# Last stage of a two-layer decoder: linears and quantised tiles batch by batch within a pair, the next pair's context part between them, bias rows added to residuals ahead of time

## What is computed

```
x = LN(x)                                              # norm 3 of the stage
x = LN1(x + Wo (Wv x + bv) + bo)                       # self-attention, whose mask leaves the diagonal; norm 4
x = LN2(x + Wm softmax(q k^T / sqrt(32)) v + bm)       # 8 heads over the context, k and v from ctx; norm 5
x3 = LN3(x + W2 relu(W1 x + b1) + b2)                  # 1024 hidden units, norm 6
x = LN(residual + x3)                                  # norm 7
gate, up = bitlinear(x, w_gate), bitlinear(x, w_up)    # 8-bit activations, ternary weights
x = LN(x + bitlinear(silu(gate) * up, w_down))         # norm 8, stored
```

## Time and profile before

| | us |
|---|---|
| median of 3 runs | 4651.4 (4647.05 to 4660.06) |
| the profiled execution | 4649.78 |
| its span | 4648.1 |
| what lies around the span | 1.7 |
| mean granted clock of PE, share of full | 0.946 |
| last stage, from the end of the state-space part (3946.5) to the end of the span | 701.6 |
| busy over the span: PE, DVE, ACT, POOL | 85%, 67%, 50%, 49% |

### The profile page before, as it was taken

The page is one execution under the profiler, slowest core; times in us unless marked ns, Lnnn a source line. Parts: engine busy times, 40 slices in busy tenths (PEclk is TensorE's granted clock), DMA queues, the critical chain, the costliest instruction groups (busy, mean ns, idle before and its releaser), DMA issues. The chain is left out here.

```text
span 4648.1 us, 46710 instructions
## 1 busy us (share of the span) xinstructions
PE 3953.6 (85%) x14986; PEld 2031.9 (44%) x14992; DVE 3108.6 (67%) x4273; ACT 2307.0 (50%) x4217; POOL 2283.4 (49%) x1206
## 2 busy tenths in 40 slices
PE   7888888888868997589999999999999987785785
PEld 3434434433438997233333333333333333434433
DVE  3464565455462111299999999999999998546546
ACT  3454444444442222476666666666666663432432
POOL 2353343344340001477877787878887785220220
PEclk9999999999989999799999999999999998898998
DMA  6000000000017886111111111111111120000000
GB/s 217 19 1 15 19 5 10 19 5 10 10 54 306 312 313 250 49 32 37 47 35 39 35 40 44 35 39 34 47 35 39 35 91 31 1 1 19 9 1 9
DMA packets 102377, 272.86 MB, mean 59 GB/s; under 512 B 9777, under 2 KB 55729, under 8 KB 96401
## 3 DMA queue, kind: packets, MB, share of 16 engines
q1 hardware_dynamic: 97216, 256.75, 16.1%
q0 software_dynamic: 4944, 13.51, 0.8%
HBM read 237.32 MB, written 32.90 MB: 58 GB/s over the span
## 5 line engine op out<-in xcount | busy, mean ns | idle before, releaser
L742 POOL TENSOR_TENSOR AR<-AR 128x1024 f32<-128x1024 f32 x512 | 1216.5, 2382 | 415.6 <-DVE AR L1852 339.1
L1852 DVE TENSOR_TENSOR_SCAN AR<-AR,PS 128x1024 f32<-128x1024 f32 x512 | 1170.6, 2286 | 17.6
L641 POOL TENSOR_TENSOR AR<-AR,rden 128x1024 f32<-128x1024 f32 x320 | 605.7, 1893 | 1121.7 <-DVE rden L1615 1055.5
L1385 PE MATMUL PS<-AR,ident 128*128 128x512 f32 x2048 | 1023.4, 627 | 32.2 <-POOL AR L742 31.7
L1005 ACT ACTIVATE AR<-AR,mcol 128x511 f32<-128x511 f32 x1024 | 668.0, 712 | 140.5 <-DVE AR L1852 138.1
L1846 DVE TENSOR_TENSOR PS<-AR,PS 128x1024 f32<-128x1024 f32 x512 | 628.1, 1227 | 78.6 <-PE PS L1370 59.6
L1385 PEld LDWEIGHTS PS<-AR,ident 128*128 128x128 f32 x2048 | 371.3, 194 | 479.2 <-issue 412.3
L1159 PE MATMUL PS<-ident,AR 128*128 128x128 f32 x2560 | 344.9, 278 | 122.1 <-issue 66.9
L1159 PEld LDWEIGHTS PS<-ident,AR 128*128 128x128 f32 x2560 | 276.5, 142 | 381.2 <-issue 360.5
L1147 PE MATMUL PS<-AR 64*128 64x512 f32 x1280 | 364.5, 650 | 50.9 <-ACT AR L806 24.0
L806 ACT ACTIVATE AR<-PS,nm 128x512 f32<-128x512 f32 x384 | 260.1, 683 | 295.4 <-DVE nm L1595 219.2
(11 more groups left out here) (266 smaller groups left out, 4726.2 us busy)
## 6 DMA issues: line engine op xcount, KB each, us to landing
AR<-in_xw SPq DMA_DIRECT2D x39, 3072.0 KB, 10.5
AR<-mid_cs SPq DMA_DIRECT2D x256, 256.0 KB, 3.3
mid_xs<-AR SPq DMA_DIRECT2D x32, 512.0 KB, 7.9
AR<-mid_xs SPq DMA_DIRECT2D x39, 128.0 KB, 9.6
mid_ys<-AR POOLq DMA_DIRECT2D x39, 128.0 KB, 7.9
AR<-in_ctx SPq DMA_DIRECT2D x8, 512.0 KB, 5.0
AR<-in_mask SPq DMA_DIRECT2D x4, 1024.0 KB, 5.3
mid_x<-AR SPq DMA_DIRECT2D x8, 512.0 KB, 3.0
```

What stands on the lines that cost most here:

```text
L641: pool.tensor_tensor(probs[:, i % 4], probs[:, i % 4], rden[:, i % 4, :].rearrange("p (q o) -> p q o", o=1).to_broadcast([P, 2, 512]), ALU ...
L742: pool.tensor_tensor(m_HC[:, W % 3], m_H[:, W % 3, :].rearrange("p (c s) -> p c s", c=2), m_cb[:, n % 4:n % 4 + 1, :].to_broadcast([P, 2, ...
L1385: ins = pe.matmul(PS[:, 2 * hf + c, :], ident[:], m_HC[:, W % 3, c, :], start=False, stop=n == NS - 1)
L1852: v.tensor_tensor_scan(m_H[:, W % 3, :], m_dA[:, W % 4].rearrange("p c s -> p (c s)"), PS[:, 4:6, :].rearrange("p c s -> p (c s)"), 0.0, A ...
```

## The change

It does five things in the last stage:

1. `sum_up` no longer adds the bias row. `with_bias` adds it to the residual, for both batches, before the products whose results are summed (`R_SAB`, `R_MHAB`, `R_LIN2B`).
2. The two linears go batch by batch on PE: first and second linear of a pair's first batch, then those of its second. Norms 6 and 7 and the quantisation of the first batch lie beside the second batch's linears.
3. In pair 0 the context part of pair 1 (transposes, keys, values) stands between the linears of b0 and of b1 on all engines. For that `f_h` moves to the space of `e_pT0` and `f_hT` behind `s_f1[0]`.
4. The 8 quantised tiles go four of the first batch and then four of the second, no longer by turns. Tile 0 stands within norm 6 of the second batch and tile 1 behind its quantisation; norm 8 of the first batch stands among the second batch's tiles.
5. SP issues ctx ahead of x2, and pair 1's ctx already after norm 5 of pair 0.

The core of the diff:

```diff
+def in_pairs(ahead, both, apart):
+    order = [(0, q, g) for g in ahead for q in range(2)]
+    for r in range(2):
+        order += [(r, q, g) for g in both for q in range(2)]
+        order += [(r, 0, g) for g in apart]
+        if r == 0:
+            order += [(1, q, g) for g in ahead for q in range(2)]
+        order += [(r, 1, g) for g in apart]
+    return order
...
-        f_h = ar([P, 4, F])
+        f_h = e_pT0.rearrange("p a c n -> p (a c n)").rearrange("p (k n) -> p k n", k=4)
...
-            pair_loads(Two(0, 1))
+            ctx_load(Two(0, 1))
+            x2_load(Two(0, 1))
...
             for p in range(2):
+                sp.wait_ge(ln_mv, LN(Two(0, p), 5) + 1)
+                ctx_load(Two(1, p))
+            for p in range(2):
                 sp.wait_ge(ln_mv, LN(Two(0, p), 7) + 1)
-                pair_loads(Two(1, p))
+                x2_load(Two(1, p))
```

ACT, after the transposes of norm 5:

```diff
-                for b in pair:
-                    for c in range(FC):
-                        pj(b, PJ_L1 + c, s_f1[b.p][:, c, :], ACT.Relu, bias=cols[:, C_L1B + c:C_L1B + c + 1])
-                for i in (6, 7):
-                    for b in pair:
-                        ln_e(b, i)
-                bit_ffn(pair)
-                for b in pair:
-                    ln_e(b, 8)
+                first_linear(pair[0])
+                for b in ahead:
+                    tr_ev(TR_CB, e_CT[b.p][:, 0, :], b)
+                ln_e(pair[0], 6)
+                for b in ahead:
+                    keys(b)
+                ln_e(pair[0], 7)
+                first_linear(pair[1])
+                ln_e(pair[1], 6)
+                hidden(pair, 0)
+                ln_e(pair[1], 7)
+                hidden(pair, 1)
+                for k in range(2, 8 + F_LAG):
+                    if k < 8:
+                        hidden(pair, k)
+                    moved_h(pair, k - F_LAG)
+                    if k - F_LAG == T - 1:
+                        ln_e(pair[0], 8)
+                ln_e(pair[1], 8)
```

PE, from the same place (`ahead` and `r == 0` mean pair 0 only):

```diff
+                tr_free(pair[0], TR_E2)
+                first_linear(pair[0])
+                second_linear(pair[0])
+                if r == 0:
+                    context((Two(1, 0), Two(1, 1)))
+                tr_free(pair[1], TR_E2)
+                first_linear(pair[1])
+                quantised(pair, 0)
+                second_linear(pair[1])
+                gate_up(pair, 0)
+                gate_up(pair, 1)
+                quantised(pair, 1)
+                for k in range(2, 8 + F_LAG):
+                    if k < 8:
+                        gate_up(pair, k)
+                    down(pair, k - F_LAG)
```

DVE:

```diff
-                own.link(v.tensor_tensor(e_R[b.p], e_R[b.p], bias_e(row), ALU.add))
+            def with_bias(b, row, src=None):
+                own.link(v.tensor_tensor(e_R[b.p], e_R[b.p] if src is None else src, bias_e(row), ALU.add))
...
+                first, second = pair
+                sum_up(first, TM_L2)
+                ln_a(first, 6, e_R[0])
+                for b in ahead:
+                    context(b)
+                ln_b(first, 6, e_R[0], R_L3G, R_L3B)
+                done(first, 6)
+                own.link(v.tensor_tensor(e_X[0], e_X[0], e_R[0], ALU.add))
+                ln_a(first, 7, e_X[0])
+                for b in ahead:
+                    values_e(b)
+                ln_b(first, 7, e_X[0])
+                done(first, 7)
+                quantised(first)
+                quantised_T(first)
+                sum_up(second, TM_L2)
+                ln_a(second, 6, e_R[1])
+                hidden(pair, 0)
+                ln_b(second, 6, e_R[1], R_L3G, R_L3B)
+                done(second, 6)
+                own.link(v.tensor_tensor(e_X[1], e_X[1], e_R[1], ALU.add))
+                ln_a(second, 7, e_X[1])
+                ln_b(second, 7, e_X[1])
+                done(second, 7)
+                quantised(second)
+                hidden(pair, 1)
+                quantised_T(second)
+                for k in range(2, 8 + F_LAG):
+                    if k < 8:
+                        hidden(pair, k)
+                    down(pair, k - F_LAG)
+                    if k - F_LAG == T - 1:
+                        v.wait_ge(f_acc, r * 8 + T)
+                        ln_a(first, 8, e_X[0])
+                    if k - F_LAG == T:
+                        ln_b(first, 8, e_X[0])
+                v.wait_ge(f_acc, r * 8 + 8)
+                ln_a(second, 8, e_X[1])
+                ln_b(second, 8, e_X[1])
+                done(second, 8)
```

More of the change, by code:

```diff
@@ L54, with __init__ @@
 class Count:
-    def __init__(self, n, p, starts=None, batches=4):
-        self.n, self.p, self.first = n, p, batches * p
-        self.starts = tuple(starts or (p,)) + (n,)
+    def __init__(self, n, p, starts=None, order=None):
+        self.n, self.p = n, p
+        starts = starts or (p,)
+        size = {g: e - g for g, e in zip(starts, starts[1:] + (n,))}
+        at, self.at = 4 * p, {}
+        for r, q, g in order or [(r, q, p) for r in range(2) for q in range(2)]:
+            for u in range(g, g + size[g]):
+                self.at[r, q, u] = at + u - g
+            at += size[g]
+        assert at == 4 * n
@@ L1041, in ln_e, with hidden @@
                 act.activation(std_e[b.p][:], mv_e[b.p][:, :, 1], ACT.Sqrt, bias=epsc[:, 0:1]).then_inc(ln_std, 1)
[L1043 to L1063, removed]
+            def hidden(pair, k):
+                b, t = pair[k // T], k % T
+                for i in range(2):
+                    n = (b.r * 8 + k) * 2 + i
+                    act.wait_ge(f_gu, n + 1)
+                    if n >= 2:
+                        act.wait_ge(f_hd, n - 1)
+                    act.activation(f_sg[:, i, :], PS[:, 2 * i, :], ACT.Silu, scale=fq[b.p][:, t, 2:3]).then_inc(f_sgd, 1)
@@ new lines, in moved_h, with keys @@
+            def moved_h(pair, k):
+                n = pair[0].r * 8 + k
+                act.wait_ge(f_ht, n + 1)
+                if n >= 4:
+                    act.wait_ge(f_o, n - 3)
+                for g in range(2):
+                    ins = act.activation(f_hT[:, n % 4, 4 * g:4 * g + 4, :],
+                                         PS[:, 4 + g, :].rearrange("p (c q) -> p c q", q=P), ACT.Copy)
+                ins.then_inc(f_hta, 1)
+            def keys(b):
+                for c in range(KC):
+                    pj(b, PJ_EK + c, s_kT[b.p][:, c, :], ACT.Identity, bias=cols[:, C_KB + c:C_KB + c + 1])
@@ L1466, in _, with context @@
+            def context(pair):
+                for b in pair:
+                    pe.wait_ge(ld_cb[b.p], (b.r + 1) * 16)
                     tr(b, TR_CB, ctx_b(b))
```

253 lines of the change are left out of this document (120 added, 133 removed).

## The result

| | before | after |
|---|---|---|
| median of the runs beside each other, us | 4651.6 (4647.1 to 4660.1) | 4625.8 (4623.4 to 4626.3) |
| ratio, 95% interval | | 0.9942 (0.9924 to 0.9959) |
| profiled execution: span, us | 4648.1 | 4623.9 |
| last stage, from its first transposes to the last norm, us | 698.1 | 672.4 |

The kernel became faster by 25.7 us between the medians, 0.55%, or 0.58% by the ratio; 4627 was forecast, within 4613 to 4638. The last row of the table is the sharper measure, and I use it from here on, as "the stage".

The account below looks back on a forecast made before the run. The stage was taken as stretches where one engine works while others stand, so laying DVE's work beside PE's gains 9.8 + 1.2 + 7.8 + 5.7 = 24.5 us: from 4649.8 to 4625.3, plus 1.6 for the median, 4627 us (4619 to 4635; with rivals 4613 to 4638).

Parts of the forecast that it names:

- Sum: Last stage, all four terms together: a gain of 9.8 + 1.2 + 7.8 + 5.7 = 24.5 us.
- Bias rows: Both attention parts: bias additions move into DVE's waits for PE, and PE's wait before output products shortens; gain 9.8 us.
- I take none of it: a wait of 2.21 us went both ways: Last output tiles: about 4 us from a faster clock behind PE's shorter wait were left out of the forecast.
- The rival of 4623: Output tiles: the clock stays up behind the shorter wait, 4 us more gain, 4623 us; chance 0.12.
- Start: Start of the stage: ctx issued ahead of x2 lands earlier for PE; gain 1.2 us, bounds 0.4 to 2.4.
- Pair 1: Pair 1, first linear to last norm: 135.1 us where it took 142.9, a gain of 7.8 us.
- Pair 0 and the seam: Pair 0's first linear to the end of pair 1's value projection: 169.0 us where it took 174.7.
- the gain of 5.7 at the seam: Pair 0 through pair 1's value projection, context part moved between pair 0's batches: 5.7 us gained.
- Order of the batches: Linears to norms and seam in both pairs, batches run one after the other: gains of 7.8 and 5.7 us.
- Table load: ACT's table switches: each load costs 1.28 us alone, its activation 0.01 us behind, without the 1.38 us drain.
- The waits of 2.4 at tiles 0 and 6: Second batch's chain: DVE waits 2.4 us for ACT's root, table load and silu at tiles 0 and 6.
- Slow tile loop: Tile loops: slow clock makes PE the bound; twelve slow tiles 4667 us, chance 0.04; four to eleven about 4648, 0.08.

Follow-up runs that it names:

- bias_back: Changed kernel with the bias rows of both attention parts added behind the sums again (second linear's stays ahead): 4639.6 us, ratio 0.9974.
- start_back: Changed kernel with x2 loaded ahead of ctx again at the start of the stage: 4618.4 us, ratio 0.9935.
- no_between: Changed kernel with the context part of pair 1 back at that pair's own start: 4623.0 us, ratio 0.9942.
- bias_alone: Kernel before with only the bias rows added in advance, for all three sums of a batch: 4626.8 us, ratio 0.9957.
- loads_doubled: Changed kernel with an extra one-column silu and root, so two more table loads, ahead of tile 0's silu in both pairs: 4634.0 us, ratio 0.9966.
- after: The changed kernel itself, first profile, against the kernel before: median 4625.8 us, ratio 0.9942.
- after_again: The changed kernel once more, unedited, beside the others on one chip: 4624.2 us, ratio 0.9940.
- moves_first: Changed kernel with ACT, in pair 1 alone, moving five banks of the second batch's first linear ahead of norm 7's root: 4620.0 us, ratio 0.9932.
- late_context: The kernel acts with pair 1's context part laid behind tile 0's gate products instead of between the batches: 4597.7 us, ratio 0.9887.
- silu_first: Changed kernel with ACT's silu ahead of norm 6's root at tile 0, and silu and moves ahead of norm 8's root, both pairs: 4614.9 us, ratio 0.9918.
- acts: Changed kernel with ACT's silus and banks ahead of roots, quantised rows' transposes within the second linear, pair 1's first norm 8 in the tail: 4605.0 us, ratio 0.9902.

## Why the prediction was right, point by point

- **Sum.** 24.5 predicted, 25.7 measured in the stage. The terms fit less well than the sum. By the experiments the bias rows of attention gave 14.6 for 9.8, the start 0 for 1.2 and all the rest 11.1 for 13.5: that their errors nearly cancelled is luck. The mechanisms, DVE's work laid into waits, were the forecast's.
- **Bias rows,** 9.8 predicted. The waits are 8 times 1.26, 10.1 us, as said, covered as said. But the edit is worth 11.35 us taken out of the changed kernel, and put alone into the one before 17.06, of which 2.5 are put down to the second linear (twice the 1.23 of a row, not measured apart): 14.6. The step that failed is "I take none of it: a wait of 2.21 us went both ways". A wait of 2.21 was followed by slow products in 7 of 8 cases over the kernel before and bias_back, and one of 0.95 by fast ones in all 40 cases of the ten profiled executions that have it. The products became 4.3 us shorter. The rival of 4623 had that mechanism with a chance of 0.12, far too little; its time was wrong all the same, since slow spots came up in the scores, the key products and the query products.
- **Start,** 1.2 predicted. PE's wait became 1.54 shorter, inside the bounds, but the stage gained 0.0 (start_back). The price of the wait was right and its worth wrong: I did not ask what the clock does behind it.
- **Pair 1,** 135.1 predicted, 136.0 measured, piece by piece, what was predicted in brackets: first linear 15.2 (15.8), norm 7's statistics at 39.4 (39.5), quantised rows at 45.2 (45.2), end of the second batch's first linear 49.0 (49.1), last sum 64.4 (64.5), DVE's chain to 91.5 (91.3), tail to 132.2 (131.4). Of the 0.9 too little, 0.2 lie ahead of the tiles and 0.6 in tiles and tail: PE stood 5.83 us for ACT's move behind the root of norm 8 and came back slow, which I had left out.
- **Pair 0 and the seam,** 169.0 predicted, 168.1 measured: the last sum came at 76.6 (78.6), since the first linear ended 0.9 earlier and PE's products behind the wait of 2.16 us for DVE's copy were not slow (7.03, against 1.0 more that I had added); 1.3 of this were lost again by norm 8. But that the context part in between is worth something, as the gain of 5.7 at the seam might be read, is wrong: no_between has the same stage. Its gain over the same stretch lies in pair 0 itself and not behind its norm 8, as the table below shows.
- **Order of the batches.** 7.8 + 5.7 = 13.5 predicted, bias rows of the linear among it. The trace beside the trace says 6.9 + 6.6. But bias_alone leaves 8.7 for all the rest, 11.1 with those rows: with the bias rows ahead, the linears of the kernel before run faster too (28.33 for 29.70 us), a gain that the comparison of two traces gives to the new order. By stretch, in us, each kernel once:

  | | stage's start to pair 0's linears | to norm 8 of pair 0 | to pair 1's linears | to the end |
  |---|---|---|---|---|
  | before | 210.4 | 142.9 | 201.9 | 142.9 |
  | bias_alone | 203.0 | 139.5 | 198.1 | 140.5 |
  | no_between | 202.6 | 136.1 | 197.9 | 135.8 |
  | changed kernel | 202.6 | 148.5 | 185.2 | 136.0 |

  From the first row to the second stand the bias rows, 17.1; from the second to the third the batches one after the other, 8.7, of which 8.1 lie in the two stretches from the linears to norm 8; from the third to the fourth the context part, nothing.
- **Table load.** 1.28, no gap: right, and shown by loads_doubled. The waits of 2.4 at tiles 0 and 6: 2.43, 2.43.
- **Slow tile loop.** It didn't come: 0.90 in the loop, tiles 5.0 us apart.

## What to carry to other kernels

Look first for small work between the last operand and the statistic that two engines wait for: moving three bias rows a batch gave 17 us, the new order of the batches 8.7. Before moving work of engine A to another place, ask how long A stands in the new place and in the old one; the context part left a stand of 11 us at the seam for a place between two linears that hid no more of it, and won 6.9 only under DVE's chain, where PE stood 13 us. And when an engine's order is written out, put next what can already run and behind it what still waits for another engine: two such swaps on ACT gave 10.5 us, somewhat more than the batch order itself.

## What the runs showed of the hardware

- Eight output products of TensorE took 1.99 us behind a stand of 0.95 us, in 40 of 40 places, and 2.9 to 3.6 behind one of 2.21 us in 7 of 8. The granted clock is at one of two levels, 2.4 or 1.2 GHz, and these are mixes of both. The length of the stand alone does not decide: behind a stand of 1.95 or 2.02 us in attention the first four score records took 1.13 us in 41 of 48 places, and only in 7 were eight of them slow (3.41).
- The slow spots repeat within 0.03 us between two executions that have the same pattern, and a time won ahead of one can move it: 2.06 us gained in one stretch came back as 1.78 lost in the next (start_back beside the changed kernel). Eight profiled executions have the same instructions from the start of the stage to the linears of pair 0 and show two patterns. Five waited 2.70 to 2.81 us for ctx (after, after_again, moves_first, no_between, late_context): last value products 6.9, query products 9.0, eight scores 3.4 us. Three waited 2.84 to 2.92 (silu_first, acts, loads_doubled): 8.5, 8.2 and no slow scores. All eight took 202.6 to 202.7 us for the whole stretch. So a difference of 0.03 us in a transfer goes with another pattern at the same sum. It isn't the wait alone: bias_back, the same up to the value products, waited 2.74 and had its key products in 7.52 us where the five took 9.1. What decides stays open.
- A table load started within 0.03 us of the end of the activation before it in 187 of 188 cases (0.37 in the other, a silu's load in acts), ahead of its own activation's wait for the products, so it costs nothing where ScalarE is idle before (15 us ahead in silu_first), and 1.3 us where the last activation of the other set is itself what one waits for.
